# Query high parts stored once and read by a repeated dimension, activation rows in three slots, and the FFN's last mask waits moved

## The reference, cut to what matters

```python
q = split_heads(input_q @ w_q)
k = split_heads(input_k @ w_k)
v = split_heads(input_v @ w_v)
scores = jnp.einsum('bhqd,bhkd->bhqk', q, k) / jnp.sqrt(jnp.float32(D_K))
scores = jnp.where(mask == 0, jnp.float32(NEG), scores)
attn = jax.nn.softmax(scores, axis=-1)
...
x = x + jnp.tanh(g_xattn[0]) * _L0_xattn_ref(_layernorm(x, axis=-1), ctx_1024, ctx_1024, ...)
x = x + jnp.tanh(g_ffn[0]) * _L0_ffn_ref(_layernorm(x, axis=-1), ...)
x = x + jnp.tanh(g_xattn[1]) * _L1_xattn_ref(_layernorm(x, axis=-1), ctx_1024, ctx_1024, ...)
x = x + jnp.tanh(g_ffn[1]) * _L1_ffn_ref(_layernorm(x, axis=-1), ...)
```

## Time and profile before

| what | before |
|---|---|
| time, median of 3 runs | 1642.17 us (1640.79 to 1644.65) |
| the profiled execution's own time | 1640.62 us |
| its span, first to last instruction | 1638.8 us |
| PE busy | 1471.2 us, 90% of the span |
| DVE, POOL, ACT busy | 66%, 55%, 50% |
| mean granted TensorE clock | 0.962 |
| DMA, 16 engines, busy by the SP queue | 42.9% |

### The profile page before, as it was taken

How to read it: one execution, slowest core, us unless ns; L and a number is a source line. 1 busy time by engine, 2 the same in 40 slices (tenths; PEclk the granted TensorE clock), 3 DMA queues, 4 the chain that set the end, 5 groups by cost and what they waited for, 6 DMA issues and landing times.

```text
span 1638.8 us, 40858 instructions
## 1 busy us (share of the span) xinstructions
PE 1471.2 (90%) x15403; PEld 1069.2 (65%) x15403; DVE 1075.1 (66%) x3588; ACT 814.1 (50%) x1908; POOL 908.2 (55%) x976
## 2 busy tenths in 40 slices
PE   0889999999999499999998789999999999659994
PEld 0457777777776255555555457777777777547773
DVE  5777777777775365665665657777777777436661
ACT  3456666666665222222222346666667666524441
POOL 0077777777776102122111267778888888744441
PEclk9999999999999699999999889999999999779997
DMA  5765445545440243222224856665566554144430
GB/s 147 194 143 104 106 105 105 105 102 106 103 88 22 59 142 87 76 75 76 76 89 125 217 100 118 117 115 112 115 130 121 119 107 94 45 153 153 146 102 8
DMA packets 215628, 176.41 MB, mean 108 GB/s; under 512 B 70154, under 2 KB 207823, under 8 KB 215432
## 3 DMA queue, kind: packets, MB, share of 16 engines
q1 hardware_dynamic: 208776, 160.35, 42.9%
q0 software_dynamic: 6656, 13.45, 2.8%
HBM read 95.86 MB, written 44.82 MB: 86 GB/s over the span
## 4 chain that ended last, share of the span: by engine, by line
PE 53%; DMA 4%; DVE 4%; POOL 2%; issue 1%; ACT 1%; SPq 1%; POOLq 0%; DVEq 0%; ACTq 0%
PE bank L1896 11%; PE bank L2084 5%; PE bank L1094 5%; PE bank L2070 5%; PE bank L1124 4%; PE bank L1142 4%; PE bank L1030 4%; PE bank L1051 4%; PE bank L1907 3%; PE bank L1173 1%; DMA q_stack_a<-max_t_a 1%; PE bank L1120 1%; DVE h0l_f L1750 1%; PE bank L582 1%; PE bank L1150 1%
## 5 line engine op out<-in xcount | busy, mean ns | idle before, releaser
L1278 ACT ACTIVATE probs_a<-bank 125x448 f32<-125x448 f32 x768 | 384.4, 540 | 17.7 <-PE bank L1124 8.5
L902 POOL TENSOR_TENSOR probs_a<-probs_a,mask_keep 125x448 int32<-125x448 int32 x256 | 285.2, 1136 | 92.6 <-ACT probs_a L1278 92.4
L1460 DVE CUSTOM_DVE_ANT_0 masked_scores_a<-bank,mask_add_a 112x375 bf16<-112x375 f32 x512 | 263.5, 552 | 111.2 <-PE bank L1094 110.6
L902 POOL TENSOR_TENSOR probs_a<-probs_a,keep_a 125x448 int32<-125x448 int32 x256 | 285.8, 1135 | 67.0 <-ACT probs_a L1278 65.1
L1460 DVE CUSTOM_DVE_ANT_0 masked_scores_a<-bank,mask_add 112x375 bf16<-112x375 f32 x512 | 260.8, 550 | 70.5 <-PE bank L1094 66.8
L1094 PE MATMUL bank<-k_stack_a,q_stack_a 96*128 96x375 f16 x1024 | 292.2, 326 | 6.3 <-DVE row_max_a L1460 5.3
L1124 PE MATMUL bank<-q_stack_a,k_stack_a 97*128 97x224 f16 x1536 | 253.2, 260 | 7.0 <-DMA q_stack_a<-max_t_a 5.9
L967 POOL TENSOR_TENSOR ctx_low_a<-ctx_in_a,ctx_high_a 128x375 f16<-128x375 f32 x128 | 113.0, 903 | 148.3 <-ACT ctx_high_a L1256 148.2
L1124 PEld LDWEIGHTS bank<-q_stack_a,k_stack_a 97*128 97x128 f16 x1536 | 146.3, 98 | 66.9 <-DMA q_stack_a<-max_t_a 7.4
L1896 PE MATMUL bank<-h0h_f,ffn_w 128*128 128x448 f16 x512 | 181.3, 354 | 3.3 <-DVE h0l_f L1750 3.3
L1896 PE MATMUL bank<-h0l_f,ffn_w 128*128 128x448 f16 x512 | 181.0, 354 | 0.0
(11 more groups left out here) (232 smaller groups left out, 3218.8 us busy)
## 6 DMA issues: line engine op xcount, KB each, us to landing
k_stack_a<-k_high_a SPq DMA_DIRECT2D x256, 96.0 KB, 4.0
ctx_in_a<-in_ctx_dram SPq DMA_DIRECT2D x64, 375.0 KB, 3.6
w_in_e<-in_L_ffn_W_dram SPq DMA_DIRECT2D x14, 1024.0 KB, 8.0
k_stack_a<-k_low_a SPq DMA_DIRECT2D x128, 96.0 KB, 4.0
q_stack_a<-q_split SPq DMA_DIRECT2D x128, 84.0 KB, 3.4
q_split<-high_a SPq DMA_DIRECT2D x32, 224.0 KB, 3.7
mask_in_f<-in_mask_BxSxS_if_dram SPq DMA_DIRECT2D x8, 656.2 KB, 7.0
mask_keep<-keep_f SPq DMA_DIRECT2D x8, 656.2 KB
```

Source lines behind the costliest of these rows:

```text
L902: pool.tensor_tensor(bits, bits, cols, ALU.mult).then_inc(masked, 1)
L1278: act.activation(probs[:, i, :], score_bank[i % 3][0:CK, 0:GT], ACT.Exp, scale=DK ** -0.5).then_inc(exped, 1)
L1460: dve.tensor_tensor_reduce(masked_scores[:, use_of[x.value, h] % 3, :], bank_of(x, h)[0:S, 0:S2], mask_add[x.four][:, 0:S2], 1.0, -LARGEST ...
```

## The change

The table `q_split` keeps only high and low. A group of queries is stored in two DMAs in place of three. A sample's queries are loaded by four DMAs in place of two: on each side the high part goes into 32 partitions by an access pattern whose source names the 16 rows twice (a leading dimension of 2 with a step of zero), and the low part into 16. Layer 1's rows have three `xg` slots, and SP loads three groups at the end of the FFN. SP's waits for the stores of the last masks move from the end of the FFN into `leave_ffn`, the first attention step of layer 1.

```diff
-    q_split = dram("q_split", [2, 3, P, B * S], F16) 
+    q_split = dram("q_split", [2, 2, P, B * S], F16) 
...
-            for g, (tile, ready) in enumerate(((self.high, self.high_ready), (self.high, self.high_ready),
-                                               (self.low, self.low_ready))):
+            for g, (tile, ready) in enumerate(((self.high, self.high_ready), (self.low, self.low_ready))):
...
-        self.xg = [sb(f"xg{n}", [S, G, D], F32) for n in range(2)]
+        self.xg = [sb(f"xg{n}", [S, G, D], F32) for n in range(3)]
...
-            if s > 1:
-                sp.wait_ge(self.turned, KC * (s - 1))
+            if s > 2:
+                sp.wait_ge(self.turned, KC * (s - 2))
...
-    q_rows = q_split.rearrange("e g (r p) (b t) -> e b (g r) p t", p=NP, t=S)
+    q_rows = q_split.rearrange("e g (r p) (b t) -> e g b r p t", p=NP, t=S)
...
             for n in range(2):
-                dst = q_view(p.four)[SIDE * n:SIDE * (n + 1), :, n * S:(n + 1) * S]
-                sp.dma_start(dst, take(q_rows[n], p.value)).then_inc(q_loaded[p.two], 16)
+                side = q_view(p.four)[SIDE * n:SIDE * (n + 1), :, n * S:(n + 1) * S]
+                high = q_rows[n, 0][p.value].unsqueeze(0).to_broadcast([2, DK, NP, S])
+                sp.dma_start(side[0:2 * DK], high).then_inc(q_loaded[p.two], 16)
+                sp.dma_start(side[2 * DK:SIDE], q_rows[n, 1][p.value]).then_inc(q_loaded[p.two], 16)
...
                 sp.wait_ge(ffn.based_stored[n], 16 * NG // 2)
+                sp.wait_ge(ffn.add_stored[n], 16 * NG // 2)
+                sp.wait_ge(ffn.keep_stored[n], 16 * NG // 2)
...
-        run_quads(3, B + LAG, sp, LOADS[done:], queries.sync, body, load_beside)
+        run_quads(3, B + LAG, sp, LOADS[4:] if layer else LOADS, queries.sync, body, load_beside)
...
                 after.queries.sync(sp, 1)
+                after.queries.sync(sp, 2)
                 after.sync(sp, opening=True)
...
-        for n in range(2):
-            sp.wait_ge(add_stored[n], 16 * NG // 2)
-            sp.wait_ge(keep_stored[n], 16 * NG // 2)
```

More of the change, by code:

```diff
@@ L46 @@
 LARGEST = 3.0e38
-FFN_SIZE, EARLY_SIZE, SPARE_SIZE = 91712, 47488, 16384
+FFN_SIZE, EARLY_SIZE, SPARE_SIZE = 91712, 51584, 16384
 CTX_SIZE = 24448
@@ L422, in vector @@
         if 0 <= q < NG:
-            wait(dve, self.stored[q % 2], 48 * (q // 2))
+            wait(dve, self.stored[q % 2], 32 * (q // 2))
             for c in range(KC):
@@ L443, in scalar @@
         if 0 <= q < NG:
-            wait(act, self.stored[q % 2], 48 * (q // 2))
+            wait(act, self.stored[q % 2], 32 * (q // 2))
             for c in range(KC):
@@ L500, in __init__ @@
         self.low = [sb(f"low{n}", [P, KC, GT], F16) for n in range(2)]
-        self.x_loaded = [sem(f"x_loaded_q{n}") for n in range(2)]
+        self.x_loaded = [sem(f"x_loaded_q{n}") for n in range(3)]
         self.turned, self.xt_high_ready, self.xt_ready = sem("turned"), sem("xt_high_ready"), sem("xt_ready")
@@ L514, in sync @@
         if s < NG:
-            if s > 1:
-                sp.wait_ge(self.turned, KC * (s - 1))
+            if s > 2:
+                sp.wait_ge(self.turned, KC * (s - 2))
             sp.wait_ge(self.ffn.stored[s % 2], 16 * (s // 2 + 1))
-            sp.dma_start(self.xg[s % 2][:, :, :], self.x_rows[s]).then_inc(self.x_loaded[s % 2], 16)
+            sp.dma_start(self.xg[s % 3][:, :, :], self.x_rows[s]).then_inc(self.x_loaded[s % 3], 16)
         r = s - 3
         if 0 <= r < NG:
-            for g, (tile, ready) in enumerate(((self.high, self.high_ready), (self.high, self.high_ready),
-                                               (self.low, self.low_ready))):
+            for g, (tile, ready) in enumerate(((self.high, self.high_ready), (self.low, self.low_ready))):
                 sp.wait_ge(ready, KC * (r + 1))
@@ L559, in tensor @@
         if 0 <= p < NG:
-            pe.wait_ge(self.x_loaded[p % 2], 16 * (p // 2 + 1))
+            pe.wait_ge(self.x_loaded[p % 3], 16 * (p // 3 + 1))
             if p == 0:
@@ L568, in tensor @@
                     last = pe.transpose(self.turn_bank[p % 2][c][:, b * S:(b + 1) * S],
-                                        self.xg[p % 2][:, b, c * P:(c + 1) * P], self.m["ident"][0:S, 0:S])
+                                        self.xg[p % 3][:, b, c * P:(c + 1) * P], self.m["ident"][0:S, 0:S])
                 last.then_inc(self.turned, 1)
@@ L832, in load_queries @@
             if p.four == 0:
-                sp.wait_ge(queries.stored[p.quad % 2], 48 * (p.quad // 2 + 1))
+                sp.wait_ge(queries.stored[p.quad % 2], 32 * (p.quad // 2 + 1))
             for n in range(2):
-                dst = q_view(p.four)[SIDE * n:SIDE * (n + 1), :, n * S:(n + 1) * S]
-                sp.dma_start(dst, take(q_rows[n], p.value)).then_inc(q_loaded[p.two], 16)
+                side = q_view(p.four)[SIDE * n:SIDE * (n + 1), :, n * S:(n + 1) * S]
+                high = q_rows[n, 0][p.value].unsqueeze(0).to_broadcast([2, DK, NP, S])
+                sp.dma_start(side[0:2 * DK], high).then_inc(q_loaded[p.two], 16)
+                sp.dma_start(side[2 * DK:SIDE], q_rows[n, 1][p.value]).then_inc(q_loaded[p.two], 16)
             if layer:
@@ L1089, in score_row @@
             if h == 0:
-                pe.wait_ge(q_loaded[x.two], 32 * (x.use2 + 1))
+                pe.wait_ge(q_loaded[x.two], 64 * (x.use2 + 1))
                 pe.wait_ge(k_loaded[x.two], 96 * (x.use2 + 1))
```

## The result

The changed kernel takes 1726.15 us (median of 4 runs, 1715.95 to 1730.71) against 1642.85 us of the kernel before beside it (1640.79 to 1644.65): a ratio of 1.050, 95% interval 1.047 to 1.052, slower. The forecast was 1699 with a range of 1652 to 1758.

A forecast was written before the change was run, and what follows sets the result against it. PE was taken as busy throughout both attentions, with no slack for the maxima's landing in attention 1. Terms 40.5 + 3 + 5 + 6 + 2 = 56.5 us on 1640.6 gave 1697, as median 1699 us; range 1652 to 1758.

The forecast's parts named there:

- PE waits in attention 1 for the first half of the maxima, 40.5 us: Attention 1, 27 steps: PE loses half the landing's lateness, 1.5 us a step; 40.5 us, bounds 0 and 53.
- lateness x = 3.0 us: Attention 1: the maxima land 3.0 us later because two engines carry 224 more packets per step; bounds 0 and 3.9.
- SP's two more issues, "hidden by SP's idle time", 0: SP's queue: two more issues per sample, 1.25 us, hidden by 2.14 us of idle time before the first maxima.
- Attention 0, 5 us: Attention 0 has 1.6 us of slack, so 0.15 us a step for 30 steps: 5 us, bounds 0 and 14.
- The clock, 3 us: Attention 1: PE waits may drop the clock to 1.2 GHz; 3 us taken, 23 if waits alternate as 3.0 and 0.
- Openings, 6 and 2: Openings of attention 1 and 0: landings behind query loads on two engines, plus SP's 1.3 in attention 1; 6 and 2 us.
- Stores, third slot, moved waits, 0: Fewer stores give nothing; PE's 3.69 us wait for the third group goes but the gain stops at DVE: 0, end -3.7.
- In attention 1 five engines are thus the late ones.: Attention 1: the 125-row mask load runs on five of 16 engines, and the maxima presumably use some of them.
- Number 4: Rival: the high load is spread over 16 engines, leaving only SP's hidden issues; 1642 to 1644 us, chance 0.08.
- Number 5: Rival, faster: load spread over 16 engines and PE's 3.69 us before attention 1 carries through; 1638 us, chance 0.05.
- rival 1: The forecast itself: high load on two engines, PE waits in attention 1; 1675 to 1725 us, chance 0.60.
- rival 2: Two engines, and worse: extra 5.8 us a step, x = 4.9, attention 0 late too; 1762 us or more, chance 0.16.

The follow-up runs named there:

- x2: The changed kernel with each side's two query loads replaced by three plain 16-row loads spread over all 16 engines: 1712.75 us, ratio 1.041.
- x6: The changed kernel with its two repeated loads of the high part issued behind the store of the first half of the maxima: 1654.53 us, ratio 1.005.
- x5: The kernel before with each side's 48-row query load split into two plain loads, 32 and 16 rows: 1669.24 us, ratio 1.014.
- x1: The kernel before with the repeated load of the high part alone; table, stores, slots and waits as before: 1737.75 us, ratio 1.057.
- x4: The changed kernel with the query table, stores and loads of before, leaving the third row slot and moved waits: 1645.88 us, ratio 1.000.
- x8: The changed kernel with the second layer's keep mask stored and loaded as 128 rows instead of 125: 1680.83 us, ratio 1.021.
- x9: The kernel before with the second layer's keep mask stored and loaded as 128 rows instead of 125: 1629.05 us, ratio 0.990.
- x7: The changed kernel with the two stores of the maxima issued by ACT in its own queue instead of by SP: 1701.96 us, ratio 1.034.

## Why the prediction was right, and where it was not

**PE waits in attention 1 for the first half of the maxima, 40.5 us.** Right in place, law and size: 39.4 us, with the alternation of long and short. But the lateness x = 3.0 us was derived from the wrong thing. The step said that 224 more packets on two engines delay the keys of those engines. In x2 the query loads give every engine the same, and the pauses are 35.1 us; in x6 the two engines have all of the packets, behind the maxima, and the pauses are 4.0. What comes late is SP: its added 3.2 us move every key store back, and the maxima with them. The traces show it step by step (means over samples 6 to 28 of attention 1): from the issue of the second half of the maxima to that of the last key it is 7.6 us before, 8.9 in x5, 10.2 in x2 and 10.9 in the changed kernel, while from that last key to PE's unit 0 it stays at 6.3, 6.2, 6.6 and 6.1 us, although the maxima are issued 2.5 us behind that key before and 1.5 in the changed kernel. That both ways give about 3 us is luck. The packets took less than forecast: where the two engines have the repeated load alone, each begins a packet every 13 ns, not 17.4, and the 224 would make 2.9 us. And SP isn't held for as long as they take, but until they begin, which is the 1.8 us that the issue behind the first repeated load of a step takes in the median.

**SP's two more issues, "hidden by SP's idle time", 0.** This step of the prediction failed. The idle time lies between the last key and the maxima, so it hides SP's lateness for the maxima's own issue, not for the keys ahead of them, on whose landing the maxima's depends. x5 prices exactly these two issues, without any repeated dimension: 23 us. The number of issues was right, but their time was wrong as well (3.2 us, forecast 1.25).

**Attention 0, 5 us.** Measured 20.6, above the bound of 14. The slack of 1.6 us was read rightly: before, the maxima land 1.75 us (median) behind their issue and are used after 3.5, and by the table some 2 us of added time are free. But the lateness over it was taken from when the last key's landing would meet the use, 0.6 us and 0.3 for the maxima; SP's 3.1 us less some 2 free ones are 1.0, half of which is near the measured 0.48 a step.

**The clock, 3 us.** 11.5 measured in attention 1, within the bound of 23. In part of the attention waits alternate as 2.7 to 3.3 and near 0, the case that the forecast left to its range. x1 has 19.5 us by the same reckoning (44.8 less 5.7, halved), so the bound was needed.

**Openings, 6 and 2.** 8.2 and 3.4. x6 still has +4.0 and +2.3. Ahead of attention 1, SP issues without a pause, and confinement isn't needed for a loss: x2 and x5, with plain loads, have +3.8 and +4.7 (though x4, with the loads of before, has +2.0 as well, which is spread). Ahead of the first unit of attention 0 the six kernels with both repeated loads need 106.1 to 108.7 us, and the eight others 101.6 to 104.9, before's 103.8 among them; so there the repeated loads count, but 3 us are also the spread between kernels that are alike there. In attention 1's opening one issue behind a repeated load took 4.87 us, at 968.25, while the stores of queries were under way.

**Stores, third slot, moved waits, 0.** Right for the slot and the waits: x4 is at 1.000, and in its profile PE no longer waits for the third group, but 11.0 us for DVE's keys, where it waited 5.2, as argued. x4 keeps all stores of before, and no run leaves out a store alone; that it is worth nothing is argued, not shown.

**"In attention 1 five engines are thus the late ones."** Right, and worth more than the prediction made of it: x8 and x9.

**The rivals.** Number 4, no confinement, said that then only SP's issues would be left, hidden. The load is confined, so the rival doesn't hold; but its sentence was wrong too: x5, two more plain issues and nothing confined, costs 1.4%, and x2, four more, 4.1%. Number 5's gain of 3.7 us did not carry through; x4 shows it. The range held the time; the sum was 27 us short, of which attention 0 is 15.6 and the clock 8.5, and the time is 1 us over what the forecast's own rival 1 allowed (1675 to 1725). The range left out rivals 4 and 5 (0.13) and nearly all of rival 2 (0.16), so its share outside was nearer 0.3 than the 0.2 stated. The sign "attention 0 within 0.2 us of its pace" came out against the forecast (14.20 against 13.52).

The Trainium skill, page "DMA: Bandwidth & Descriptors", section "Rules for kernel authors", has the rule that an outermost dimension under 16 confines a DMA to at most as many engines, and a dimension of a multiple of 16 should stand outermost. Both sides of it agree: the share of 0.17 and the 3 updates of the repeated load, and 1% of the kernel's time for three rows of padding in x9. What the runs add is that the dearer part of the confined load here was not its own landing but the issue behind it, and that even unconfined the added issues keep four fifths of the loss (67 of 83 us in x2).

## What to carry to other kernels

An issuing engine's idle time is no cover for more issues unless everything issued ahead of that idle time has slack too: ask which landing the last awaited transfer shares its engines with, and count from the first issue that is pushed back. Put loads that are needed late behind the store that is needed next, whatever their form; order alone cut the loss from 83 to 8 us. And look at the outermost dimension of every DMA, the old ones too: a mask of 125 rows cost this kernel 1% before anything was changed.

## What the runs showed of the hardware

In the changed kernel the issue of the DMA that follows a load confined to two engines took at least 0.98 us, 1.32 in the median and up to 4.87, against 0.6 for the same DMA behind a load spread over all; behind a plain load of the same size (x5) the median was 0.6. It ended 0.3 us (median) after the confined load's first packets had begun; in the longest case these began 4.5 us behind their issue, while the other engines were busy with stores of queries, and it ended 1.1 us later. It strikes whichever DMA is next: in x6 the output's store, 1.57 us in the median against 0.33.

A small transfer issued from another engine's queue still needed 4.2 us in the median beside the key stores of attention 1 (x7), where the second half of the maxima in attention 0 of the changed kernel took 1.7, issued when the key stores had landed.

Steps with equal pauses in total can lose different work to the clock: 28.6 and 44.8 us at the 1.2 GHz level for 40.5 and 42.4 us of pauses. A pause alone does not tell whether the clock falls: in attention 1 of the changed kernel 3.4 us at 1.2 GHz stand behind six of the eight pauses of 2.7 to 4.0 us and behind one of the six of 1.5 to 2.5.
